# Expert stage of a four-block stack: the two tokens of a pair gathered by two products from halves of the rows, weighted one-hots without zeros

## The reference

```python
q = (xn @ w_q.T).reshape(b, s, 2, NH, KD)...          # xn: batch-normed inputs
sim = einsum('bpnhd,hkpd->bpnhk', q, keys_p)           # two sides of 32 keys, 8 heads
scores, idx = top_k(sim, K)                            # 8 best per side
all_scores = scores[0][..., :, None] + scores[1][..., None, :]
all_idx = idx[0][..., :, None] * NK + idx[1][..., None, :]
sc, pk = top_k(all_scores, K)                          # 8 best of 64 pairs
indices = take_along_axis(all_idx, pk)                 # expert numbers, 0 .. 1023
hmid = einsum('bnd,bnhkd->bnhk', inputs, down[indices])
hmid = sigmoid(sc) * gelu(hmid)
out = einsum('bnhk,bnhkd->bnd', hmid, up[indices])
```

## Time and profile before

| | us |
|---|---|
| median of 3 runs | 583.02 (580.79 to 585.88) |
| the profiled execution, its own time | 583.85 |
| its span in the trace | 582.1 |
| mean granted clock of TensorE | 0.745 |
| stage `peer` in the span | from 311 to 582 |
| busy in the span | DVE 482.1, PE 411.8, ACT 314.8, POOL 182.2 |

### The profile page before, as it was taken

One profiled execution on the slowest core, in us unless ns is written; L12 is line 12 of the kernel. 1 busy time (PEld: TensorE's weight loads), 2 busy tenths in 40 slices (PEclk: granted clock), 3 DMA queues, 4 the chain that ended last, 5 costly groups with the idle time before them and its releaser, 6 DMA issues. The chain is left out here.

```text
span 582.1 us, 12503 instructions
## 1 busy us (share of the span) xinstructions
PE 411.8 (71%) x4564; PEld 293.6 (50%) x4564; DVE 482.1 (83%) x2076; ACT 314.8 (54%) x643; POOL 182.2 (31%) x208
## 2 busy tenths in 40 slices
PE   1778868987999699956746345868657675855575
PEld 0555447644765477625642123546445353724475
DVE  4576869699869987898963998799979999989991
ACT  0601376418542664236421639586786868588590
POOL 4450133933194318613513132103030303030000
PEclk9987978797967986776556855775868585958576
DMA  7210000000000000000000000000000000000000
GB/s 213 78 46 0 1 2 2 1 2 0 2 1 2 1 1 2 2 0 1 2 1 0 1 1 1 3 2 11 3 11 1 11 3 9 3 10 2 11 2 19
DMA packets 12459, 6.72 MB, mean 12 GB/s; under 512 B 3182, under 2 KB 11758, under 8 KB 12398
## 3 DMA queue, kind: packets, MB, share of 16 engines
q1 hardware_dynamic: 10566, 4.34, 2.7%
q10 hardware_dynamic: 1832, 1.58, 0.8%
HBM read 4.87 MB, written 1.05 MB: 10 GB/s over the span
## 5 line engine op out<-in xcount | busy, mean ns | idle before, releaser
L1738 ACT ACTIVATE hot_last<-iota_f,lo_last 128x128 f16<-128x128 f32 x256 | 75.8, 391 | 0.3 <-DVE lo_last L1862 0.3
L2000 PE MATMUL psum<-hot_w,hot_lo 128*128 128x16 f16 x1536 | 43.3, 172 | 15.1 <-DVE hot_lo L1879 15.1
L1879 DVE TENSOR_TENSOR hot_lo<-lo_t,iota_lo 128x4096 f16<-128x4096 f16 x24 | 53.6, 2287 | 0.3
L1966 PE MATMUL psum<-x3t,down_t 128*128 128x512 f32 x64 | 43.8, 789 | 13.3 <-ACT hid L1704 11.6
L2000 PEld LDWEIGHTS psum<-hot_w,hot_lo 128*128 128x128 f16 x1536 | 41.7, 101 | 21.5 <-DVE hot_lo L1879 19.8
L1652 POOL TENSOR_TENSOR eq<-eq,side_f 128x1024 f16<-128x1024 f16 x14 | 28.9, 2083 | 55.5 <-DVE eq L1840 55.5
L1329 PE MATMUL psum<-q_hi,k_t 32*128 32x128 f16 x256 | 36.5, 260 | 9.1 <-DVE masked L905 7.9
L2000 PE MATMUL psum<-hot_w,hot_last 128*128 128x16 f16 x512 | 14.8, 174 | 38.7 <-issue 31.2
L1660 POOL TENSOR_TENSOR rstd<-rstd,minus_half 128x2 f32<-128x2 f32 x8 | 5.6, 702 | 115.0 <-DVE rstd L1909 115.0
L1809 DVE FIND_INDEX8 side_i<-side,keysims 128x8 uint32<-128x32 f32 x256 | 41.5, 185 | 0.0
L1250 PE MATMUL psum<-we,x1t 128*128 128x512 f32 x64 | 40.3, 777 | 0.4 <-DVE z L842 0.4
(11 more groups left out here) (271 smaller groups left out, 1194.5 us busy)
## 6 DMA issues: line engine op xcount, KB each, us to landing
xall<-in_L_attn_x SPq DMA_DIRECT2D x4, 256.0 KB, 6.2
out<-o SPq DMA_DIRECT2D x8, 128.0 KB, 2.8
we<-in_L_ffn_We SPq DMA_DIRECT2D x1, 512.0 KB, 4.3
downn<-in_L_ffn_down SPq DMA_DIRECT2D x1, 512.0 KB, 5.2
upw<-in_L_ffn_up SPq DMA_DIRECT2D x1, 512.0 KB, 6.3
wh<-in_L_attn_W_h SPq DMA_DIRECT2D x1, 256.0 KB, 4.2
keysn<-in_L_ffn_keys_p ACTq DMA_DIRECT2D x1, 256.0 KB, 9.4
wqkv<-in_L_attn_w_qkv ACTq DMA_DIRECT2D x1, 192.0 KB
```

Source lines behind the costliest of these rows:

```text
L1738: ins = nc.scalar.activation(hot_last[:, lane], iota_f[:], ACT.Abs, bias=lo_last[:, lane:lane + 1], scale=-1.0)
L1879: nc.vector.tensor_tensor(hot_lo[:, pairs], bc(lo_t[:, lanes].rearrange("p (j s) -> p j s", s=2).unsqueeze(2), [P, LB // 2, P, 2]), bc(v.i ...
L1966: nc.tensor.matmul(bank[H_BANK(b, c)][:], v.down_t[:, c, :], v.x3t[:, N * b:N * b + N], start=True, stop=True).then_inc(h_mm.h, 1)
L2000: ins = nc.tensor.matmul(bank[2 + q][:, c:c + 2 * EH], low, hot_w[:, i, lane // 2, :, :, lane % 2].rearrange("p t e -> p (t e)"), start=(i ...
```

## The change

The 16 columns per lane become 8. For every lane the two tiles of the pair are gathered apart: one product takes rows 0 to 63 (first tile), another rows 64 to 127 (second tile), and they write into two banks, 2 + t for the lanes of quarters 0 and 1 and 4 + t for those of quarters 2 and 3. `hot_w` has no zeros any more, so each of its two products runs once over all 128 rows. `mix` reads two banks at once and therefore waits for both quarters of a bank pair; the scale of 4096 moves into the `up` table, which POOL multiplies once.

```diff
-        hot_w = sb("hot_w", [P, 2, P // 2, 2, EH, 2], F16)
+        hot_w = sb("hot_w", [P, 2, P // 2, EH, 2], F16)
...
+        upw_ok = sem("upw_ok")
...
-                nc.gpsimd.memset(lo_shift[:], HI_BASE * P)
-                nc.gpsimd.memset(hot_w[:], 0.0).then_inc(zeroed.h, 1)
+                nc.gpsimd.memset(lo_shift[:], HI_BASE * P).then_inc(zeroed.h, 1)
                 for u in (0, 1):
                     candidates(u)
+
+                arrived(pool, "peer")
+                nc.gpsimd.tensor_scalar(v.upw[:], v.upw[:], 1.0 / WEIGHT_SCALE, None, ALU.mult).then_inc(upw_ok.h, 1)
...
-                    for t in range(2):
-                        q = slice(HK * t, HK * t + HK)
-                        for i, w in enumerate((w_hi, w_lo)):
-                            ins = nc.vector.tensor_tensor(
-                                hot_w[q, i, :, t], hot_hi[q],
-                                bc(w[q].rearrange("p (j s) -> p j s", s=2).unsqueeze(2), [HK, P // 2, EH, 2]),
-                                ALU.mult)
+                    for i, w in enumerate((w_hi, w_lo)):
+                        ins = nc.vector.tensor_tensor(
+                            hot_w[:, i], hot_hi[:],
+                            bc(w[:].rearrange("p (j s) -> p j s", s=2).unsqueeze(2), [P, P // 2, EH, 2]), ALU.mult)
...
-                        wait(dve, g_mm, p, q + 1)
+                        wait(dve, g_mm, p, q // 2 * 2 + 2)
...
-                        nc.vector.scalar_tensor_tensor(
-                            mix[:, :, lanes], bank[2 + q][:].rearrange("p (l e) -> p e l", e=2 * EH), 1.0 / WEIGHT_SCALE,
-                            hid[:, b % 2, at:at + 2, :, lanes].rearrange("p t e l -> p (t e) l"),
-                            ALU.mult, ALU.mult).then_inc(mix_ok.h, 1)
+                        columns = slice(EH * LB * (q % 2), EH * LB * (q % 2 + 1))
+                        nc.vector.tensor_tensor(
+                            mix[:].rearrange("p (t e) l -> p t e l", t=2)[:, :, :, lanes],
+                            v.psum[:, 2 + q // 2 * 2:4 + q // 2 * 2, columns].rearrange("p t (l e) -> p t e l", e=EH),
+                            hid[:, b % 2, at:at + 2, :, lanes], ALU.mult).then_inc(mix_ok.h, 1)
...
-                        wait(pe, mix_ok, p - 1, q + 1)
+                        wait(pe, mix_ok, p - 1, q // 2 * 2 + 2)
                     for lane in range(LB * q, LB * q + LB):
-                        low = hot_lo[:, lane // 2, :, lane % 2] if q < QB - 1 else hot_last[:, lane - LB * q, :]
                         for i in range(2):
-                            c = 2 * EH * (lane % LB)
-                            ins = nc.tensor.matmul(
-                                bank[2 + q][:, c:c + 2 * EH], low,
-                                hot_w[:, i, lane // 2, :, :, lane % 2].rearrange("p t e -> p (t e)"),
-                                start=(i == 0), stop=(i == 1))
+                            for t in range(2):
+
+                                half, c = slice(HK * t, HK * t + HK), EH * (lane % (2 * LB))
+                                low = hot_lo[half, lane // 2, :, lane % 2] if q < QB - 1 else hot_last[half, lane - LB * q, :]
+                                ins = nc.tensor.matmul(
+                                    bank[2 + q // 2 * 2 + t][:, c:c + EH], low, hot_w[half, i, lane // 2, :, lane % 2],
+                                    start=(lane % (2 * LB) == 0 and i == 0), stop=(i == 1), skip_group_check=True)
...
-                arrived(pe, "peer")
+                pe.wait_ge(upw_ok.h, 1)
```

## The result

| | before | changed |
|---|---|---|
| median of 4 runs | 581.9 (579.79 to 585.88) | 594.76 (592.56 to 595.01) |
| profiled execution: time, span | 583.85, 582.1 | 592.56, 590.8 |
| end of one last gather to the end of the next, pairs 1 to 5 | 29.61, 32.41, 29.79, 30.49, 31.45 | 31.85, 30.60, 31.86, 32.74, 31.94 |
| the same, pairs 6 and 7 | 24.65, 23.70 | 26.76, 22.74 |
| last gather itself, pairs 0 to 7 | 1.86 to 1.87 in all | 1.87, **4.01**, 1.87, **3.84**, 1.88, **3.93**, **3.36**, **3.75** |

What follows compares the result with a forecast made beforehand. Bound: a loop through TensorE and ScalarE, not VectorE. -1.29 + 0.15 + 0.59 + 0.59 = +0.04 us gave 583.9 from the profiled execution, 583.1 from the median; forecast 583.5, range 580.5 to 599, its own 580.5 to 587.

Steps and rivals of the forecast that it cites:

- The bound: Closed loop from last gather to last gather through TensorE and ScalarE, 29.6 to 32.4 us in pairs 1 to 5; VectorE follows.
- Weighted one-hots: VectorE's two instructions for four save 1.29 us per pair, but lie on the path only in pair 6: -1.29.
- Rival 3: VectorE's saving does reach the loop: 10.3 us less, 573; chance 0.07.
- Mixes: Second mix behind the last gather: +0.15 over three faster loop turns, +0.59 at pair 5's end, +0.59 in pair 7.
- The sign that I had given: VectorE's idle time before m2 should be about 1.3 + 0.6 us larger per pair than before m3 previously.
- POOL: Its new 128 x 1024 multiplication fits where POOL sat idle 8.55 us, even at twice half of 4.12: 0.
- Gather: TensorE's quarter of 128 half-row products overlaps and stays at 1.87 us, within bounds of 1.87 and 3.60: 0.
- the 2.7 us that I had named as a sign of being wrong: The forecast is wrong if the last quarter of the gather is longer than 2.7 us.
- Rival 1: Gather halves don't overlap, one product per 27 ns: 10.4 us more in pairs 0 to 5, 598 in all; chance 0.22.
- the rival's +3.9: Without overlap, pair 7's four gather quarters end at 572.9 where before it was 569.03: +3.9 us.

Runs made afterwards that it cites:

- e4: Kernel before with two weighted one-hot instructions of 128 rows instead of four (second tile's weights left out), mixes waiting as before; 583.81 us, ratio 0.996.
- e9: Kernel before with ScalarE writing 24 lanes of low one-hots instead of 32, VectorE 104, its fourth-quarter lanes gathered ahead of the key score; 576.29 us, ratio 0.988.
- e3: Kernel before with two weighted one-hot instructions of 128 rows instead of four (second tile's weights left out) and mixes waiting in pairs; 581.07 us, ratio 0.996.
- e2: Kernel before with each gather product of 16 columns split into two of 8, both on all 128 rows and into the same bank; 606.83 us, ratio 1.041.
- e1: Changed kernel without the gather products for the weights' low half, 64 half-height products a quarter instead of 128; 584.17 us, ratio 1.000.
- e5: Changed kernel with 95, 103 and 97 unused weight loads ahead of the last quarter in pairs 1, 2 and 5; 591.28 us, ratio 1.012.
- e8: Changed kernel with ScalarE writing 24 lanes of low one-hots instead of 32, VectorE 104, its fourth-quarter lanes gathered ahead of the key score; 573.82 us, ratio 0.983.

## Why the forecast of no difference failed, point by point

- **The bound** (loop through TensorE and ScalarE): right. e4 turned 9.9 of 10.3 us into waiting; moving 8 lanes off ScalarE gave 1.2% (e9).
- **Weighted one-hots, -1.29 in pair 6**: right; -1.4 in the turn from pair 6 to pair 7 of e4's trace, and -2.2 in its time (0.38% of 585.2, between -4.4 and -0.1). Rival 3 (573) is out.
- **Mixes, +0.15 + 0.59 + 0.59**: right at the two ends, +0.61 and +0.59 between the traces of e4 and e3, and 0.00 in place of +0.15 in the loop; the times alone could not tell. The sign that I had given, 1.3 + 0.6 us more idle time per pair, was misread: VectorE's idle time in a turn is the turn less its work, and a mix that moves behind the wait adds none. e3's wait is 24.7 against e4's 23.6 over all pairs, where 0.6 a pair would have been 4.8.
- **POOL, 0**: right. 2.79 us against an estimate of twice a half of 4.12, with 5.67 us idle left behind it.
- **Gather, 0**: this is the step that failed. The value came out (1.87 in pairs 0, 2 and 4), the term did not. I priced a quarter as if only its products counted, and took one duration for all eight pairs. It came out as two: 1.87, and 3.4 to 4.0 where the next block of instructions had not been called for in time. Five of eight quarters stopped, all over the 2.7 us that I had named as a sign of being wrong, and four of them were on the path: 6.2 us in pairs 1, 3 and 5, and 1.9 in pair 7, 8.1 in place of 0. Pair 6's 1.5 cost nothing, since its mixes did not wait. I had the number at hand: the page of before gives 36 packets for instructions, and I read no timing of that queue. The value itself had luck in it: rows 8 have eight products in 0.24 us, 30 ns each, so they show two strips at work at once, but a supply of one product per 27 ns on average would have let them through just the same. They were no evidence for 13.4 ns.
- **Rival 1** gave 598 and named the supply of instructions as its possible ground. Its time was near, its mechanism is refuted: quarters of 3.6 in every pair are e2's, not the changed kernel's. A supply of one instruction per 13 ns would have stretched each quarter; what there is comes by blocks, and it lets a quarter through or holds it 2 us. In pair 7, four quarters now take 12.5 us (564.46 to 576.96) against 9.1, close to the rival's +3.9. The Trainium skill's "TensorE: Matmul & The Clock Gate", section "Wait — 56ns, not 53.3ns?", would allow no start within 25 ns of the last: e2 agrees for products on the same rows (27 ns), the changed kernel does not for products on different halves (13.4 ns).

## What to carry to other kernels

Before splitting work into more, smaller instructions, count them against the supply: here 256 instructions, once TensorE had no other work, came no faster than every 3.5 to 3.6 us, however well the products overlapped, and where TensorE stops depends on how far into a block it was before its last wait, so it hits some iterations and not others. A mean per line hides it (the mean product is 164 or 165 ns in the changed kernel, in e1, e5 and e8 alike); compare the duration of the same group in every iteration. And what an engine off the bound is spared is worth nothing until work is moved onto it; rebalance first, then count the saving.

## What was not expected of the hardware

- 128 products of 64 rows, 128 columns of weights and 8 moving columns ran in 1.87 us with their weight loads, in alternation on the two halves of the rows: 13.4 ns from one to the next, half of the 27 ns of the same on 128 rows (64 in 1.87, e2's 128 in 3.56). Whether it moves 8 or 16 columns makes no difference there.
- TensorE's instructions arrive in packets of 256 (16 more packets for 4096 instructions). While TensorE is dense, resumptions lie 3.54 and 3.59 us apart (pair 7), with stops of 1.7 to 2.0 us in the last quarters (1.3 in pair 6). The packet shows about 1 us after TensorE goes on past a point that lies between some 70 instructions (pair 5, not called) and some 110 (pair 5 of e5, called) into the block, and what counts is the instructions that stand ahead of a wait, executed or not. Why only one block is called ahead, and whether the point is a fixed count, stays open.
